# The root of the first attention's mean squares, for 14 more batches on VectorE instead of GpSimd

## The reference, cut to what matters

```python
q = (x @ w_q).reshape(B, S, N_HEADS, HEAD_DIM)      # 16 heads of 8
k = (x @ w_k).reshape(B, S, N_KV, HEAD_DIM)         # 4 heads of 8
q = x * lax.rsqrt(mean(square(x), -1) + 1e-5)       # _rms_norm, of q and of k
...                                                 # rope, tanh cap, causal softmax, @ v
x = _layernorm(x + y @ w_o)
x = _layernorm(x + ffn(x))     # layernorm, attention of 16 heads, layernorm,
                               # one of 8 experts (128 -> 512 -> 128) per token
```

## Time and profile before

| | |
|---|---|
| median of 3 runs | 716.66 us (716.57 to 719.5) |
| time of the profiled execution | 709.74 us |
| its span, first to last instruction | 708.0 us, 15104 instructions |
| busy, share of the span | PE 77%, DVE 69%, ACT 59%, POOL 59% |

### The profile page before, as it was taken

How to read it: one execution, slowest core, us unless ns; L and a number is a source line. 1 busy time by engine, 2 the same in 40 slices (tenths; PEclk the granted TensorE clock), 3 DMA queues, 4 the chain that set the end, 5 groups by cost and what they waited for, 6 DMA issues and landing times.

```text
span 708.0 us, 15104 instructions
## 1 busy us (share of the span) xinstructions
PE 545.2 (77%) x5145; PEld 319.9 (45%) x5145; DVE 486.6 (69%) x1356; ACT 421.1 (59%) x650; POOL 417.1 (59%) x442
## 2 busy tenths in 40 slices
PE   2547687888787878778786888787886989777893
PEld 1223242444333444334343554445452556556893
DVE  3545847779758886686869878687767667745453
ACT  1675155677864665765686584847584636453561
POOL 2468664588573954575668486858463216334574
PEclk9968678899987978896989899797997879998997
DMA  6400020000000000000002130100000402167650
GB/s 146 133 7 2 1 77 2 1 24 18 9 1 25 24 2 1 25 16 9 1 25 62 48 97 17 36 25 6 5 34 15 122 5 66 41 222 215 188 168 14
DMA packets 30138, 34.22 MB, mean 48 GB/s; under 512 B 6970, under 2 KB 21984, under 8 KB 30064
## 3 DMA queue, kind: packets, MB, share of 16 engines
q1 hardware_dynamic: 26096, 25.53, 12.6%
q0 software_dynamic: 2816, 6.43, 2.5%
q10 hardware_dynamic: 1152, 1.30, 0.6%
HBM read 22.37 MB, written 11.27 MB: 48 GB/s over the span
## 4 chain that ended last, share of the span: by engine, by line
PE 40%; DVE 21%; issue 12%; POOL 12%; ACT 11%; SPq 1%; DMA 1%; POOLq 0%; ACTq 0%; DVEq 0%
DVE mx L1180 9%; PE out L827 6%; ACT p L923 4%; ACT p L954 3%; PE out L712 3%; PE ring_s L793 3%; PE ring_p L893 3%; POOL rs L1360 3%; PE ring_s L813 3%; PE ring_p L764 3%; ACT p L927 2%; POOL stack L1363 2%; PE ring_p L881 2%; PE ring_p L771 2%; PE ring_s L699 2%
## 5 line engine op out<-in xcount | busy, mean ns | idle before, releaser
L1180 DVE TENSOR_REDUCE mx<-ring_s 128x4 f32<-128x1024 f32 x128 | 151.9, 1217 | 25.1 <-PE ring_s L793 24.6
L954 ACT ACTIVATE p<-ring_s 128x1024 f32<-128x1024 f32 x128 | 125.4, 1028 | 29.3 <-PE ring_s L813 28.6
L923 ACT ACTIVATE p<-ring_s 128x1024 f32<-128x1024 f32 x96 | 97.1, 1025 | 38.5 <-PE ring_s L699 38.3
L1379 POOL TENSOR_SCALAR_AFFINE_SELECT p<-p 128x512 f32<-128x512 f32 (+1 forms) x96 | 77.0, 809 | 57.9 <-ACT p L927 57.7
L1363 POOL TENSOR_SCALAR stack<-stack 128x256 f16<-128x256 f16 (+1 forms) x96 | 65.0, 700 | 69.6 <-DVE stack L1078 36.6
L1360 POOL TENSOR_TENSOR rs<-ms,small 128x40 f32<-128x40 f32 x14 | 94.9, 6775 | 12.7 <-DVE ms L1043 12.3
L927 ACT ACTIVATE p<-p 128x1024 f32<-128x1024 f32 x96 | 100.2, 1059 | 0.3
L793 PE MATMUL ring_s<-kc,qs 32*128 32x256 f16 x512 | 53.8, 302 | 28.3 <-DVE mx L1180 16.9
L827 PE MATMUL out<-p,v 128*32 128x256 f32 x1024 | 73.8, 418 | 1.6 <-DVE rb L1238 1.3
L813 PE MATMUL ring_s<-qs,kc 32*128 32x256 f16 x512 | 47.2, 294 | 13.9 <-ACT p L954 10.0
L712 PE MATMUL out<-p,v 128*32 128x256 f32 x512 | 51.3, 480 | 7.1 <-DVE ve L1133 2.6
(11 more groups left out here) (157 smaller groups left out, 1090.4 us busy)
## 6 DMA issues: line engine op xcount, KB each, us to landing
w_up<-in_L_ffn_w SPq DMA_DIRECT2D x40, 256.0 KB, 2.7
t_row<-routed_rows SPq DMA_DIRECT2D x40, 132.0 KB, 2.3
routed_rows<-padrow SPq DMA_DIRECT2D x8, 396.0 KB, 3.1
xs<-in_L_attn_x SPq DMA_DIRECT2D x16, 128.0 KB, 2.2
routed_rows<-padrow SPq DMA_DIRECT2D x8, 132.0 KB, 1.9
qs<-mT SPq DMA_DIRECT2D x64, 2.0 KB
out<-t_y,t_idx POOLq DMA_INDIRECT x40
b_down<-in_L_ffn_b SPq DMA_DIRECT2D x1, 512.0 KB, 5.0
```

The lines of the kernel that those rows point to most:

```text
L923: nc.scalar.activation(p1[:, u], bank(f"b_sc{u}", n)[:], ACT.Tanh, scale=float(ISQ / CAP)).then_inc(b_s.sem, 1)
L954: nc.scalar.activation(p2[:, u], bank(f"e_sc{u}", n)[:], ACT.Exp, scale=float(ISQ)).then_inc(e_s.sem, 1)
L1180: nc.vector.tensor_reduce(mx2[:, t, 2 * pair:2 * pair + 2, 2 * k:2 * k + 2], bank(f"d_mx{j}", n)[:].rearrange("p (z g s) -> p z g s", z=2, ...
L1379: nc.gpsimd.affine_select(out=w, in_=w, compare_op=ALU.is_ge, fill=0.0, base=0, pattern=[[0, w.shape[1]], [1, P]], channel_multiplier=-1). ...
```

## The change

ROOTS goes from 2 to 16: all batches take a_root on DVE, and no batch takes a_pow on POOL. Beside this the ranks in ORDER are other ones for nearly all steps of all engines. Nothing else differs; DVE has 14 x 11 = 154 instructions more, POOL 14 fewer. Line numbers after L128 are lower by one in the changed kernel.

```diff
-ROOTS = 2
+ROOTS = 16
 ONLY = dict(a_root=tuple(range(ROOTS)), a_pow=tuple(range(ROOTS, B)), p_bT=(0,), p_bTc=(0,), p_plan=tuple(last for last, *_ in PLANS), q_sp=(PLANS[-2][0],))
 ORDER = {
...
-    "a_root": (17, 35),
...
-    "a_pow": (79, 138, 219, 338, 471, 596, 756, 873, 981, 1115, 1261, 1353, 1508, 1606),
...
+    "a_root": (13, 32, 97, 153, 241, 374, 484, 618, 756, 900, 1016, 1148, 1256, 1400, 1525, 1649),
```

More of the change, by code:

```diff
@@ new lines @@
+    "a_load": (0, 1, 3, 4, 16, 209, 316, 416, 554, 658, 768, 913, 959, 1244, 1317, 1457),
+    "a_xT": (2, 10, 17, 60, 135, 235, 349, 480, 610, 748, 860, 998, 1110, 1255, 1341, 1505),
+    "a_xTc": (5, 6, 12, 73, 161, 250, 386, 513, 655, 759, 864, 1012, 1138, 1257, 1345, 1512),
+    "a_qkv": (7, 15, 59, 117, 205, 326, 448, 569, 701, 835, 938, 1069, 1169, 1338, 1493, 1585),
+    "a_rope": (8, 20, 51, 118, 207, 340, 460, 583, 704, 837, 968, 1068, 1217, 1336, 1496, 1601),
+    "a_stack": (9, 35, 99, 174, 227, 390, 490, 624, 773, 924, 1017, 1180, 1286, 1416, 1541, 1665),
@@ new lines @@
+    "d_kT": (124, 217, 324, 462, 599, 714, 841, 960, 1080, 1229, 1378, 1517, 1621, 1772, 1905, 2017),
+    "d_stack": (125, 196, 311, 489, 577, 696, 816, 947, 1063, 1213, 1351, 1520, 1604, 1738, 1890, 2011),
+    "p_bT": (134,),
+    "d_qTc": (138, 222, 309, 472, 615, 719, 827, 976, 1082, 1240, 1376, 1532, 1616, 1764, 1896, 2030),
+    "d_kTc": (141, 226, 344, 470, 605, 727, 845, 980, 1093, 1233, 1382, 1533, 1633, 1780, 1899, 2028),
[3 rows of a table added]
+    "p_bTc": (157,),
[13 rows of a table added]
+    "d_nm": (198, 296, 394, 530, 670, 792, 898, 1029, 1142, 1291, 1453, 1640, 1730, 1867, 1956, 2076),
@@ new lines @@
+    "f_place": (356, 474, 604, 728, 830, 973, 1096, 1218, 1349, 1559, 1694, 1808, 1925, 2010, 2095, 2184),
+    "f_rank": (357, 467, 596, 721, 820, 966, 1072, 1195, 1355, 1545, 1684, 1787, 1924, 2008, 2099, 2170),
+    "f_res": (362, 517, 654, 743, 811, 965, 1109, 1203, 1420, 1599, 1653, 1788, 1957, 2024, 2088, 2163),
+    "f_scatter": (404, 614, 712, 755, 957, 1083, 1184, 1219, 1537, 1702, 1709, 1805, 2007, 2075, 2115, 2193),
+    "p_plan": (1221, 1809, 2098, 2188),
+    "g_row": (1223, 1267, 1277, 1299, 1308, 1342, 1447, 1487, 1521, 1783, 1810, 1835, 1871, 1874, 1992, 2001, 2006,
+        2121, 2131, 2137, 2168, 2173, 2196, 2205, 2209, 2223, 2225, 2228, 2245, 2247, 2266, 2274, 2299, 2304, 2319,
+        2329, 2331, 2336, 2348, 2357),
@@ new lines @@
+    "g_w": (1242, 1278, 1292, 1298, 1343, 1396, 1440, 1489, 1516, 1774, 1793, 1834, 1870, 1949, 1988, 1995, 2092,
+        2104, 2110, 2166, 2176, 2182, 2189, 2199, 2202, 2210, 2229, 2232, 2251, 2255, 2265, 2286, 2305, 2317, 2322,
+        2335, 2337, 2350, 2363, 2375),
+    "g_hT": (1247, 1258, 1365, 1397, 1436, 1538, 1596, 1647, 1771, 1826, 1917, 1960, 1967, 1990, 2053, 2056, 2061,
+        2140, 2145, 2172, 2179, 2190, 2216, 2217, 2236, 2239, 2244, 2262, 2271, 2292, 2294, 2300, 2313, 2315, 2324,
+        2339, 2343, 2364, 2379, 2389),
@@ new lines @@
+    "g_hTc": (1252, 1273, 1367, 1425, 1434, 1547, 1611, 1644, 1766, 1830, 1928, 1958, 1966, 2005, 2060, 2062, 2071,
+        2144, 2154, 2175, 2177, 2187, 2208, 2215, 2234, 2246, 2248, 2257, 2270, 2284, 2298, 2310, 2320, 2325, 2346,
+        2352, 2366, 2370, 2383, 2398),
+    "g_up": (1265, 1271, 1387, 1534, 1590, 1626, 1650, 1741, 1785, 1914, 1948, 1974, 2002, 2042, 2065, 2085, 2101,
+        2153, 2161, 2180, 2191, 2195, 2218, 2227, 2238, 2258, 2264, 2276, 2289, 2295, 2301, 2311, 2326, 2328, 2338,
+        2356, 2374, 2384, 2393, 2394),
@@ new lines @@
+    "g_mid": (1266, 1274, 1405, 1544, 1603, 1625, 1659, 1737, 1804, 1921, 1945, 1983, 2013, 2048, 2063, 2077, 2117,
+        2156, 2158, 2185, 2200, 2206, 2226, 2230, 2249, 2254, 2263, 2277, 2283, 2308, 2312, 2321, 2332, 2347, 2359,
+        2369, 2377, 2385, 2400, 2402),
+    "g_down": (1350, 1372, 1463, 1540, 1656, 1725, 1743, 1762, 1816, 1931, 1994, 2026, 2037, 2084, 2111, 2128, 2136,
+        2162, 2181, 2194, 2214, 2224, 2237, 2250, 2259, 2267, 2287, 2290, 2306, 2307, 2318, 2333, 2341, 2353, 2373,
+        2376, 2388, 2397, 2401, 2409),
@@ new lines @@
+    "g_rs": (1353, 1483, 1522, 1554, 1677, 1723, 1742, 1802, 1883, 1919, 2025, 2040, 2044, 2114, 2142, 2147, 2155,
+        2203, 2204, 2212, 2221, 2231, 2242, 2253, 2268, 2278, 2280, 2285, 2309, 2340, 2345, 2349, 2361, 2365, 2371,
+        2380, 2391, 2403, 2404, 2410),
+    "g_z": (1361, 1373, 1467, 1560, 1671, 1735, 1746, 1777, 1853, 1959, 1999, 2033, 2041, 2089, 2109, 2125, 2143,
+        2174, 2192, 2201, 2213, 2233, 2235, 2256, 2261, 2272, 2273, 2288, 2302, 2314, 2327, 2334, 2354, 2358, 2378,
+        2382, 2392, 2399, 2405, 2412),
@@ new lines @@
+    "g_y": (1392, 1503, 1568, 1643, 1674, 1744, 1778, 1790, 1894, 2027, 2031, 2082, 2094, 2106, 2127, 2139, 2169,
+        2197, 2198, 2207, 2219, 2240, 2241, 2260, 2269, 2281, 2296, 2297, 2316, 2330, 2344, 2351, 2355, 2372, 2386,
+        2390, 2396, 2406, 2408, 2414),
+    "g_out": (1504, 1584, 1628, 1695, 1708, 1856, 1935, 1969, 2021, 2036, 2087, 2141, 2149, 2152, 2159, 2183, 2186,
+        2211, 2220, 2222, 2243, 2252, 2275, 2279, 2282, 2291, 2293, 2303, 2323, 2342, 2360, 2362, 2367, 2368, 2381,
+        2387, 2395, 2407, 2411, 2413),
@@ L282 @@
+    "q_sp": (2133,),
 }
```

144 lines of the change are left out of this document (45 added, 99 removed), and 122 rows, old and new, of the table ORDER.

## The result

The changed kernel takes 743.62 us (median of 4 timed runs, 742.84 to 745.1) against 717.48 us (4 runs, 716.57 to 719.5) for the kernel before in the same session. The ratio is 1.0363, with a 95% interval of 1.0333 to 1.0393. The direction was forecast, the size was not: 724.8 us was predicted, with 708 to 737 as the range. The loss is three times the predicted one.

What follows compares the result with a forecast made beforehand. The prediction took many short waits between engines in a fixed order, none full, to bound the kernel. Its terms, +9.6 +3.9 +1.0 -3.7 -2.7 = +8.1 us on 716.66, gave 724.8 us, range 708 to 737.

Steps and rivals of the forecast that it cites:

- Removed from POOL: Fourteen powers, 94.9 us, leave POOL; most had no one waiting, so the gain was put at -3.7 and -2.7 us.
- -3.7 for `qn`'s wait: DVE's 11.9 us of idle time waiting for the power, times 0.31, saved.
- -2.7 for what stood behind the power: POOL steps queued behind the power: 0.8 us in batch 2, as much in two more, something for the scatters.
- Added on DVE: Fourteen roots of eleven instructions, 2.54 us each with gaps, 35.6 us in all, charged +9.6 and +3.9 us.
- I take 3 us: Busy time the roots on DVE lose to collisions with POOL's masks; 0.31 of it counts, +1 us.
- The bound of 12.2 us: Most that collisions with POOL's masks could cost the roots on DVE: 14 x 0.87 us.
- The share that counts, 0.42 and 0.31: Chain time over busy time as the price of added DVE time: 0.42 in series of maxima, 0.31 at DVE's mean.
- Nine roots in series of maxima: Nine of fourteen DVE roots lie within a series of maxima and delay it: 9 x 2.54 x 0.42 = 9.6 us.
- The other ranks: The changed order of every engine, put at nothing, with a few us either way in the range.
- Absorbed: Rival: DVE's 114.3 us of idle time take up the roots, gains and costs cancel, 716.7 us; chance 0.24.
- GpSimd was the bound: Rival: three powers on the chain are its only path, each replaced by a root, 12.7 us gained, 704.0 us; chance 0.24.
- DVE becomes the bound: Rival: every DVE root costs its length less the idle time replaced, +23.7 us, 740.4 us; chance 0.10.

Runs made afterwards that it cites:

- e4: Kernel before with the power of batches 2 to 15 replaced on POOL by one cheap multiply and add; ratio 0.9912.
- e11: Kernel before plus one long spare DVE instruction per batch directly behind the split in batches 2 to 15; ratio 1.0389.
- e5: Kernel before, powers kept, plus eleven spare DVE instructions directly behind the split of batches 2 to 15; ratio 1.0518.
- e5b: Kernel before, powers kept, plus eleven spare DVE instructions directly behind the negated maxima of batches 0 to 13; ratio 1.0513.
- e1: Kernel before in its own order, with all roots on DVE directly ahead of their splits and no power on POOL; ratio 1.0387.
- e8: Kernel before with the roots of batches 4, 7, 13 and 14 also on DVE, POOL's power for the others from batch 2; ratio 1.0018.
- f2: Changed kernel with two Newton steps in place of three, eight instructions per root; ratio 1.0101.
- e10: Kernel before plus a spare power of 13 columns on POOL behind each stack of batches 2 to 15; ratio 1.0315.
- g6: Kernel before with the input transposes of batches 2 to 15 made four times each on PE; ratio 1.0112.
- e9: Kernel before plus three spare copies on ACT per batch, behind the cast of the maxima of batches 0 to 13; ratio 1.0354.

## Why the prediction was wrong

*What bounds the kernel.* Right as far as it went: many short waits between engines in a fixed order. It drew the wrong consequence from it, below.

*Removed from POOL, -6.4 us.* Right in size. e4 gave -6.4 us with an interval of -9.3 to -3.5. How it splits into -3.7 for `qn`'s wait and -2.7 for what stood behind the power was not measured, and the -3.7 uses the same share, 0.31, that failed for the added work. That the sum agrees to the tenth is luck.

*Added on DVE, 35.6 us of length.* Mis-sized. 43 us, since a root is 3.0 us in company and not 2.54. This is worth 5 to 7 us of the result at the charge found. "I take 3 us" for the collisions was the mis-sized number, 7.4 us against it. The bound of 12.2 us held for the total, but not the 0.87 us for a root that it was made of: batch 8's root lost 2.4 us and batch 15's 1.9 us.

*The share that counts, 0.42 and 0.31.* This is the step that failed. The prediction took an engine's part of the chain over its busy time as the price of a microsecond more on it. Measured by spare work in before's order, the price is 0.75 to 0.92 on DVE, at either place, in one piece or eleven, for half the amount as well. With the chain's share the added work came to 14.5 us; with the gain of e4 taken off the result, it was 26.1 + 6.4 = 32.5 us for 43 us, or 0.76. That this is what e11 has is in part a coincidence: at eight instructions the same sum gives 7.2 + 6.4 = 13.6 us for 30.2 us, or 0.45, near the prediction's share. So no single fraction would have been right. A reading that fits, but that no run isolates: the share says what fraction of the existing work lies on the path that ended last, and added work lengthens every path of nearly that length through the engine as well. The same would make removing so cheap: with 92 us off POOL another path of nearly the same length is next. The prediction itself saw that second path beside the powers of batches 5 and 6, and used it only for the saving.

*Nine roots in series of maxima, +9.6 us.* That the place makes them dearer is refuted by e5 and e5b, in before's order. What was to show it, more than 42.8 us of waits of `ring_s` loads behind `mx` in the middle, hardly came there (43.8 us); over the whole span they grew from 46.5 to 56.4 us. The test was no measure of the cost either way. In e5b, whose spare work stands behind the maxima, these waits are what they were in before, and it still costs 36.7 us:

```profile
PEld ring_s L799 <- DVE mx L1206: 34.2, 48, 2.0
...
PEld ring_s L705 <- DVE mx L1206: 12.8, 18, 1.6
```

*The other ranks, nothing.* At eleven instructions they measure as nothing: 1.0363 against 1.0387 for e1, whose intervals overlap. That is a coincidence of this length, as the table of lengths shows.

*The rivals.* "Absorbed" and "GpSimd was the bound" are refuted, the latter by e4: powers that cost almost nothing give 6.4 us (9.3 at most), so no root could have given 12.7. Batches 4, 7, 13 and 14 do absorb their roots (e8, to within 3.4 us). "DVE becomes the bound" came nearest with 740.4 us, and its arithmetic, length less the idle time replaced, is close to right. Its reason is not shown. The Trainium skill ("Perfetto Trace Analysis", Identifying the Most-Contended Engine) has the engine of highest occupancy as the one to relieve; beside the runs here occupancy does not tell the price, since a microsecond on ACT at 59% costs about as much as one on DVE at 69% (0.92 against 0.75 to 0.92). DVE at 82% of the middle, which was to set it off, never came: it stayed at 76%.

*What stays open.* PE's busy time grew in all slowed kernels with the same 5145 matmuls, by 11 us (f2) to 32 us (e5b), at a mean granted clock of 0.81 to 0.85 where the profiled execution of before has 0.867. Part of the charge may come by this way. An estimate of how much: among the executions of before, which differ in clock by themselves, 0.01 less goes with 2.3 to 4.1 us more, by session; after's four executions (0.824 to 0.828) are some 0.028 below before's median of 0.854, which would make 6 to 11 of the 26 us. Whether the clock is there the cause of the time or follows from the waits, no run tells. It is not the whole of it: e1 and e11 cost 3.9% with PE at 558.6 and 559.8 us, while e10 costs 3.2% with 568.7. And g6, whose clock is that of before, costs 0.70. The runs don't separate the two. The profiled execution of before was 7.7 us below the median here, so some of the difference in PE's time may be that of the execution.

## What to carry to other kernels

In a pipeline of several engines in a fixed order, an engine's share of the chain is no price. Here spare work of 12 to 46 us cost 0.65 to 0.92 of its length on any of four engines, and 92 us taken away gave 6.4 us. Neither is a constant: roots that replace listed waits cost nothing that can be measured, and in the changed order one stretch of root time cost 0.22 of its length and the next 1.5. Where the price matters, put spare work of the same length on the engine and time it: here e11 and e4 together, +27.8 and -6.4 us, come to +21.4 where the change cost 26.1. No other kernel was measured.

## What the runs showed of the hardware

The mean granted clock was lower with spare work on DVE, ACT or POOL. The 71 executions of before that stand beside the experiments have 0.835 to 0.869, with a median of 0.854; the four of e11 have 0.825 to 0.841, those of e9 0.824 to 0.835, those of e10 0.831 to 0.838. With spare work on PE it was not lower: a median of 0.851 in g6, where before has 0.853. One fall in after, with a root in it (PE, PEld, DVE, ACT, POOL, then the clock):

```profile
370.00:374.40 4.40, 2.96 (x30) 1.50 (x26) 3.62 (x4) 2.81 (x5) 0.00 (x0) 1.00 0.01 4
374.40:376.50 2.10, 1.39 (x10) 0.45 (x6) 2.03 (x5) 0.97 (x2) 2.00 (x3) 0.50 0.00 0
376.50:380.50 4.00, 2.30 (x10) 1.07 (x8) 3.65 (x12) 3.92 (x7) 2.19 (x4) 0.50 0.01 2
380.50:391.40 10.90, 8.33 (x62) 3.65 (x62) 6.09 (x21) 5.37 (x7) 7.94 (x11) 0.50 0.07 26
391.40:400.00 8.60, 6.78 (x82) 4.22 (x84) 7.14 (x27) 6.40 (x8) 5.75 (x9) 1.00 0.01 2
```

PE had been busy 2.96 of 4.4 us, and the clock went to 0.50, that is from 2.4 to 1.2 GHz, and back to 1.00 at 391.4 us. The fall is not the root's doing: it came at 374.4 us, and the root starts at 376.52. On the chain the same eight matmuls stand at either level:

```profile
383.07 1.08 PE out L711 x8
...
396.02 0.57 PE out L711 x8
```

In before, the clock also falls near the same step, `nm` of batch 8 at 354.44, but it is back after 7 us, not 17:

```profile
356.00:363.00 7.00, 5.77 (x50) 3.70 (x50) 4.25 (x17) 5.85 (x8) 4.26 (x7) 0.51 0.07 20
```

So matmuls that follow a time in which PE waited can take twice their time. Whether the root prolonged this fall, and how much of the charge comes by this way, is not known.

A short instruction of DVE can be held by POOL for its whole length. The eleven take 0.18 to 0.20 us alone. In after one of `guess`, with a single input, took 0.75 us, and the `root` behind it 1.02 us; over the sixteen batches the two-input group with `ms` has a mean of 269 ns. DVE, then POOL, in batch 11:

```profile
376.81 0.75 DVE L1050 TENSOR_SCALAR guess<-guess 128x40 int32<-128x40 int32 x1
377.60 1.02 DVE L1055 TENSOR_TENSOR root<-guess 128x40 f32<-128x40 f32 x1
...
376.80 0.72 POOL L1397 TENSOR_TENSOR x1b<-x,b_out 128x256 f32<-128x256 f32 x1
377.48 1.09 POOL L1378 TENSOR_SCALAR_AFFINE_SELECT p<-p 128x1024 f32<-128x1024 f32 x1
```

The Trainium skill ("SBUF — State Buffer", Who interferes with whom) says that the one that issues second waits for the end of the first, and the rows of batches 11 and 15 agree to 0.1 us, for POOL's two-input sums and for its mask. The longest case doesn't fit that order: in batch 8 a `root` started at 255.71 and took 1.82 us, to the end of a mask on POOL that started only at 256.36 (1.10 us). In the root of batch 15 a scaling with one input on POOL (`x`, 519.74 to 521.35) let three instructions of 0.20 us pass.
